# A two-layer Flamingo block on one core: the split context kept in DRAM between the layers

## The reference

```
layer 0: q, k, v = per-head 8x8 products of x, ctx, ctx     (16 heads of width 8)
         a = softmax(where(mask == 0, -1e20, q k^T) / sqrt(128));  h = a v Wo^T + bo
         x = x + tanh(g_xattn[0]) * h
         y = layernorm(x);  x = x + tanh(g_ffn[0]) * (shared_swiglu(y) + routed_swiglu(y, top 1 of 8))
layer 1: q = y Wq^T + bq,  k, v = ctx Wkv^T + bkv            (16 heads of width 64)
         x = x + tanh(g_xattn[1]) * (softmax(q k^T / 8) v Wo^T + bo)
         x = x + tanh(g_ffn[1]) * ffn(layernorm(x))          (ternary weights, 8-bit activations, width 512)
```

## Time and profile before

| | |
|---|---|
| median of 3 runs (lowest to highest) | 1311.85 us (1311.23 to 1313.99) |
| the profiled execution's own time | 1311.5 us |
| its span in the profile | 1309.6 us |
| PE busy / DVE / ACT / POOL | 87% / 70% / 55% / 43% of the span |
| DMA bytes moved | 137.91 MB |

### The profile page before, as it was taken

The page is one execution under the profiler, slowest core; times in us unless marked ns, Lnnn a source line. Parts: engine busy times, 40 slices in busy tenths (PEclk is TensorE's granted clock), DMA queues, the critical chain, the costliest instruction groups (busy, mean ns, idle before and its releaser), DMA issues.

```text
span 1309.6 us, 27739 instructions
## 1 busy us (share of the span) xinstructions
PE 1133.5 (87%) x10078; PEld 646.3 (49%) x10080; DVE 923.1 (70%) x1252; ACT 716.4 (55%) x983; POOL 560.2 (43%) x360
## 2 busy tenths in 40 slices
PE   0869899999999996887968899899999999999974
PEld 0335566566665655533424454544545454454542
DVE  6656666666666664777787767678686767777768
ACT  0525455555555545545666666566665656666642
POOL 5357766666666724234034323333333333333220
PEclk9979899999999999899999999999999999999996
DMA  5233334433443351000049878868677786867630
GB/s 157 71 91 82 82 97 106 119 80 101 107 112 81 83 146 38 1 21 27 1 73 141 147 154 141 161 135 156 135 148 154 139 156 136 162 135 136 119 68 14
DMA packets 256726, 137.91 MB, mean 105 GB/s; under 512 B 229184, under 2 KB 239920, under 8 KB 256672
## 3 DMA queue, kind: packets, MB, share of 16 engines
q1 hardware_dynamic: 250416, 134.03, 49.1%
q10 hardware_dynamic: 6256, 3.16, 1.0%
HBM read 49.64 MB, written 0.52 MB: 38 GB/s over the span
## 4 chain that ended last, share of the span: by engine, by line
PE 55%; DVE 12%; issue 9%; DMA 7%; SPq 6%; ACT 6%; ACTq 3%; POOL 1%; DVEq 0%; another core or an unknown queue 0%; POOLq 0%
PE bank L854 9%; PE bank L872 8%; PE bank L718 7%; PE bank L742 6%; DMA region<-u_w 5%; PE bank L746 5%; PE bank L759 4%; SPq L452 4%; PE bank L820 3%; DMA region<-wg_sb 3%; ACTq L384 3%; DVE region L1713 2%; DVE e_row L1522 2%; DVE neg_max L1561 2%; ACT region L1205 2%
## 5 line engine op out<-in xcount | busy, mean ns | idle before, releaser
L1522 DVE CUSTOM_DVE_ANT_0 e_row<-bank,region 112x1500 f32<-112x1500 f32 x128 | 220.1, 1720 | 125.4 <-PE bank L718 124.1
L1561 DVE TENSOR_REDUCE neg_max<-bank 128x1 f32<-128x1500 f32 x112 | 192.3, 1717 | 139.9 <-PE bank L854 139.9
L1205 ACT ACTIVATE region<-bank 125x896 f32<-125x896 f32 x192 | 176.0, 917 | 203.1 <-PE bank L746 203.0
L854 PE MATMUL bank<-region 128*128 128x500 f16 x1008 | 233.5, 377 | 3.3 <-ACT e_row L1232 1.8
L1241 ACT COPY region<-bank 128x768 f16<-128x768 f16 x224 | 178.2, 795 | 105.2 <-PE bank L820 105.2
L1232 ACT ACTIVATE e_row<-bank,neg_shift 128x1500 f32<-128x1500 f32 x112 | 169.4, 1513 | 84.5 <-DVE neg_shift L1565 84.3
L536 POOL CAST u_w<-e_row 128x1500 f16<-128x1500 f32 x56 | 81.8, 1461 | 210.9 <-ACT e_row L1232 210.9
L536 POOL CAST wg_sb<-e_row 128x1500 f16<-128x1500 f32 x56 | 82.5, 1473 | 201.4 <-ACT e_row L1232 156.5
L854 PEld LDWEIGHTS bank<-region 128*128 (+1 forms) x1008 | 96.8, 98 | 106.8 <-ACT e_row L1232 2.3
L742 PE MATMUL bank<-row_of,region 112*128 112x448 bf16 x384 | 138.1, 360 | 7.9 <-ACT region L1205 7.9
L746 PE MATMUL bank<-region 97*128 (+1 forms) x768 | 137.8, 260 | 0.0
(11 more groups left out here) (222 smaller groups left out, 1610.2 us busy)
## 6 DMA issues: line engine op xcount, KB each, us to landing
c_in<-in_ctx SPq DMA_DIRECT2D x32, 750.0 KB
region<-region SPq DMA_DIRECT2D x64, 192.0 KB, 2.8
region<-in_mask_Bx1xSxS_if SPq DMA_DIRECT2D x32, 328.1 KB
region<-region SPq DMA_DIRECT2D x64, 96.0 KB, 2.6
region<-region SPq DMA_DIRECT2D x8, 750.0 KB
g_w<-region SPq DMA_DIRECT2D x8, 750.0 KB
x_norm_t<-inverse_rows SPq DMA_DIRECT2D x16, 256.0 KB, 3.6
x_norm_t<-inverse_rows SPq DMA_DIRECT2D x16, 192.0 KB, 3.6
```

The costliest lines, as they stand in the source:

```text
L854: last = pe.matmul(score_banks1(par, t)[:, k, :], q1[:, ql, b, 128 * t:128 * (t + 1)], c_t1[par][:, cl, 4 * k:4 * k + 4, 0:KP], start=(ql ...
L1205: act.activation(p0[:, 2 * i:2 * i + 2, :], ring0("s", h, i)[0:KP, :, 0:HALF_ROWS], ACT.Exp, scale=SCALE0)\
L1522: dve.tensor_tensor_reduce(out=masked.rearrange("p (a k) -> p a k", a=3), in0=bank[0:R0, 0:3, 0:4 * KP], in1=mask_bias[par][:].rearrange(" ...
L1561: dve.tensor_reduce(neg_max[:, t:t + 1], score_banks1(par, t), AX.XY, ALU.max, negate=True)\
```

## The change

**Layer 0.** `c_split0` is laid out with all high columns of a chunk side by side, then all low ones. SP stores it, 750 KB a batch, to a DRAM scratch `split_rows` (`sync_split_out`, ahead of the load for batch b+2), and POOL's next split waits for that store. Each turned bank is now one half of all four groups, so a group needs both banks; the stacks are 12 DMAs of 32 rows, 8 after the first bank and 4 after the second, where they were 8 DMAs (64 and 32 rows); the bytes are the same.

**Layer 1.** The second load from `ctx`, ACT's and POOL's split, PE's 24 turns and DVE's two copies are gone. Instead `sync_split_in` loads both halves of batch b+2 from the scratch into `c_split1` at slot 3, and `sync_keep` loads those of batch b+1 from the scratch into `c_keep1` at slot 4, where it stood before. The context transpose of batch b+1 is issued ahead of slot 0 instead of after slot 2. The inverse's steps of both groups stand one slot earlier on PE and ACT (slots 4 and 0), and those of group 0 on SP too.

```diff
-        c_split0 = carve([128, KC, G, 2, 32], F16)
+        c_split0 = carve([128, KC, 2, G, 32], F16)
+        split_rows = nc.dram_tensor("split_rows", [B, KP, KC, 2, E], F16, kind="Internal").ap()
...
         def sync_stack(sp, b, par):
             wait_apart(sp, "sp", (sem("st0"), (b - 1) * (2 * NP)))
-            for g in range(G):
-                if g % 2 == 0:
-                    wait_apart(sp, "sp", (sem(f"ct_done0_{g // 2}"), b + 1))
-                rows = 64 * (g % 2)
-                sp.dma_start(c_stack[par][0:64, g], c_t0[rows:rows + 64, g // 2]).then_inc(sem(f"stack{par}_{g}"), 16)
-                sp.dma_start(c_stack[par][64:96, g], c_t0[rows:rows + 32, g // 2]).then_inc(sem(f"stack{par}_{g}"), 16)
+            for n in range(2):
+                wait_apart(sp, "sp", (sem(f"ct_done0_{n}"), b + 1))
+                for g in range(G):
+                    for at in ((0, 64), (32,))[n]:
+                        sp.dma_start(c_stack[par][at:at + 32, g], c_t0[32 * g:32 * g + 32, n])\
+                            .then_inc(sem(f"stack{par}_{g}"), 16)
+
+        def sync_split_out(sp, b):
+            wait_apart(sp, "sp", (sem("low0"), b + 1))
+            sp.dma_start(split_rows[b], c_split0[0:KP].rearrange("p c n g d -> p c n (g d)")).then_inc(sem("split_out0"), 16)
+
+        def sync_split_in(sp, b):
+            wait_apart(sp, "sp", (sem("c_turned1"), 16 * b))
+            sp.dma_start(c_split1[0:KP], split_rows[b]).then_inc(sem("split_in1"), 16)
...
         def sync_keep(sp, b, par):
-            wait_apart(sp, "sp", (sem("split_done1"), b + 1))
             wait_apart(sp, "sp", (sem("pv_done1"), 4 * (b - 1)))
-            sp.dma_start(c_keep1[par], c_split1[0:KP]).then_inc(sem("kept1"), 16)
+            sp.dma_start(c_keep1[par], split_rows[b]).then_inc(sem(f"kept1_{par}"), 16)
...
             def layer1(b, par, first, last):
-                if not (isinstance(b, int) and b + 2 >= B):
-                    sync_load_context(sp, 1, b + 2, par)
+                if not last:
+                    sync_turn_context1(sp, b + 1, 1 - par)
                 for t in range(T1):
                     sync_turn1(sp, b, par, t)
                     if t == 1 and not first:
                         sync_inverse_out1(sp, b - 1, 1 - par, 1)
                     if t == 2 and not first:
                         sync_inverse_back1(sp, b - 1, 1 - par, 1)
+                    if t == 4:
+                        sync_inverse_out1(sp, b, par, 0)
                     if t == 5:
-                        sync_inverse_out1(sp, b, par, 0)
-                    if t == 6:
                         sync_inverse_back1(sp, b, par, 0)
-                    if t == 2 and not last:
-                        sync_turn_context1(sp, b + 1, 1 - par)
+                    if t == 3 and not (isinstance(b, int) and b + 2 >= B):
+                        sync_split_in(sp, b + 2)
                     if t == GROUPS1[1][0] and not last:
                         sync_keep(sp, b + 1, 1 - par)
...
             low_weights(1)
             pool_rstd(pool, 1, TT, (0, TT))
-            pool_context1(pool, 0, 0)
             low_weights(2)
...
             def layer1(b, par, first, last):
                 for t in range(T1):
                     pool_high1(pool, b, par, t)
-                    if t == 2 and not last:
-                        pool_context1(pool, b + 1, 1 - par)
...
                 for t in range(T1):
-                    if t == 1 and not first:
+                    if t == 0 and not first:
                         act_inverse1(act, b - 1, 1)
-                    if t == 5:
+                    if t == 4:
                         act_inverse1(act, b, 0)
-                    if t == 1 and not last:
-                        act_split1(act, b + 1, 1 - par)
```

More of the change, by code:

```diff
@@ L223, in flamingo_kernel @@
         assert at[0] == split_at
-        c_split1 = carve([128, 2, KC, E], F16)
-        c_keep1 = [carve([128, 2, KC, E], F16)[0:KP],
+        c_split1 = carve([128, KC, 2, E], F16)
+        c_keep1 = [carve([128, KC, 2, E], F16)[0:KP],
                    g_w[:].rearrange("p e i -> p (e i)")[0:KP, 0:KC * E].bitcast(F16)
-                   .rearrange("p (n c e) -> p n c e", c=KC, n=2)]
-        c_t1 = [carve([128, 2, KC, 128], F16) for _ in range(2)]
+                   .rearrange("p (c n e) -> p c n e", c=KC, n=2)]
+        c_t1 = [carve([128, KC, 2, 128], F16) for _ in range(2)]
         GROUPS1 = [(0, 4), (4, T1)]
@@ L482, in layer0 @@
                         sync_load_mask(sp, b + 2)
+            sync_split_out(sp, 0)
             sync_stack(sp, 0, 0)
@@ L714, in pe_rows0 @@
             if t % 2 == 0:
-                pe.wait_ge(sem(f"stack{par}_{t // 2}"), per_use(b, par, 32))
+                pe.wait_ge(sem(f"stack{par}_{t // 2}"), per_use(b, par, 48))
             wait(pe, sem("max_done0"), b * T0 + t)
@@ L789, in pe_prep0 @@
                 last = pe.transpose(into[:, 128 * c:128 * (c + 1)],
-                                    c_split0[:, c, 2 * n:2 * n + 2].rearrange("p g two d -> p (g two d)"), ident16[:])
+                                    c_split0[:, c, n].rearrange("p g d -> p (g d)"), ident16[:])
             last.then_inc(sem("ct_turned0"), 1)
-        def pe_prep(pe):
-            for n in range(2):
-                pe.wait_ge(sem("split_done1" if n else "high1"), 1)
-                for c in range(KC):
-                    last = pe.transpose(pair_flat(n, F16)[:, 128 * c:128 * (c + 1)], c_split1[:, n, c, :], ident16[:])
-                last.then_inc(sem("ct_turned1"), 1)
         def projected1():
@@ L839, in pe_inverse1 @@
             pe.wait_ge(sem("inv_done1"), b * T1 + z)
-            pe.wait_ge(sem("high_copied1"), 2 * (b * T1 + (T1 if grp == 1 else GROUPS1[0][1])))
+            pe.wait_ge(sem("high_copied1"), 2 * (b * T1 + (T1 - 1 if grp == 1 and not (isinstance(b, int) and b == B - 1)
+                                                            else T1 if grp == 1 else 3)))
             if grp == 0 and isinstance(b, int) and b == B - 1:
-                pe.wait_ge(sem("residual"), 2 * TT + EARLY)
+                pe.wait_ge(sem("residual"), 2 * TT + 4)
             pe.transpose(inverse_turned()[0:z - a], row_inv[:, par, a:z], ident[:]).then_inc(sem("inverse_turned1"), 1)
@@ L846, in pe_scores1 @@
             if t == 0:
-                if isinstance(b, int) and b == 0:
-                    pe.wait_ge(sem("ct_done1"), 2)
-                else:
-                    pe.wait_ge(sem("c_turned1"), b * 16)
+                pe.wait_ge(sem("c_turned1"), 16 * (b + 1))
             wait(pe, sem("exp_done1"), b * T1 + t - 1)
@@ L868, in pe_pv1 @@
                 if grp == 0:
-                    pe.wait_ge(sem("kept1"), (b + 1) * 16)
+                    pe.wait_ge(sem(f"kept1_{par}"), per_use(b, par, 16))
             for c in range(first, end):
                 for cl, pl in ((0, 0), (0, 1), (1, 0)):
-                    last = pe.matmul(bank[:, U_BANK, 0:cols], c_keep1[par][:, cl, c, :], p1[grp][0:KP, pl, c, :],
+                    last = pe.matmul(bank[:, U_BANK, 0:cols], c_keep1[par][:, c, cl, :], p1[grp][0:KP, pl, c, :],
                                      start=(c == 0 and cl + pl == 0), stop=(c == KC - 1 and cl == 1))
@@ L1249, in act_inverse1 @@
             act.copy(inverse_row[0:z - a], inverse_turned()[0:z - a]).then_inc(sem("inverse_row1"), 1)
-        def act_split1(act, b, par):
-            act.wait_ge(sem(f"ctx_in1_{par}"), per_use(b, par, 16))
-            if not (isinstance(b, int) and b == 0):
-                act.wait_ge(sem("ct_turned1"), 2)
-                wait(act, sem("c_turned1"), 16 * (b - 1))
-                act.wait_ge(sem("kept1"), 16 * b)
-            act.copy(c_split1[0:KP, 0], c_in[par][:]).then_inc(sem("high1"), 1)
         def act_context0(act, b, par, n, place):
@@ L1262, in act_context0 @@
             if not (isinstance(b, int) and b == 0):
-                for g in (2 * n, 2 * n + 1):
-                    act.wait_ge(sem(f"stack{1 - par}_{g}"), per_use(b - 1, 1 - par, 32))
+                for g in range(G):
+                    act.wait_ge(sem(f"stack{1 - par}_{g}"), per_use(b - 1, 1 - par, 48))
             act.copy(c_t0[:, n].rearrange("p c k -> p (c k)"),
```

66 lines of the change are left out of this document (28 added, 38 removed).

## The result

| | before | after |
|---|---|---|
| median of the runs (lowest to highest) | 1312.31 us (1311.23 to 1313.99, 4 runs) | 1339.81 us (1332.96 to 1342.30, 4 runs) |
| the profiled execution's own time | 1311.5 us | 1342.3 us |
| its span | 1309.6 us | 1340.6 us |

The changed kernel is slower: the ratio is 1.020, with an interval of 1.0161 to 1.0239. The interval lies clear of 1, but whether the loss is more or less than 2% it leaves open. The forecast was 1279, with a range of 1258 to 1298.

A forecast was written before the change was run, and what follows sets the result against it. PE was taken to bound layer 1, with 5.6 us of waits per pair of batches. From 1311.5, layer 1 net -29.3 (-49.3 + 20.0), first FFN -3.3 and layer 0 nothing gave 1278.9, said as 1279; range 1258 to 1298.

The forecast's parts named there:

- The gain of layer 1: Layer 1: three waits vanish, 3.17 us in each of batches 2 to 14 (41.2) and 6.3 in batch 1.
- The wait inside `neg_shift`: Layer 1, slot 3: DVE's one-column addition waits 1.91 us during POOL's subtraction; removing it gains 1.80 us a batch.
- ACT's cast: Layer 1, slot 1: the context cast (1.47 us) stands ahead of copy and exponential; removing it gains .51 us a batch.
- the wait for turned tile 3: Layer 1: PE waits for tile 3's low half, its transpose queued behind the context's; removing this gains .86 us a batch.
- Tile 4's transpose lands at about 31.9, and tile 6's low half needs it at 31.7: the edge: Layer 1, us after slot 0's start: the transpose is .2 late, within the slack, so it costs nothing.
- Stalls after even batches too: Layer 1, a sign of error: if DVE's DMA wait stands after even batches too, the time is 1290 and more.
- the forecast's pattern: Layer 1: tile 5's transpose is 3.7 us late after odd batches only; PE loses 2.85 each, 7 x 2.85 = 20.0.
- I take 0: Layer 0: no net change, the new stacks and the 750 KB store being covered.
- The first FFN's start: DVE's seven normalizations lose POOL's subtraction beside them and end sooner; gain 3.3 us, between 0 and 5.4.
- PE's 24 turns ... give nothing; where they were on it, it would only be more gain: First FFN: batch 0's removed turns lie beside ACT's chain, so no gain; if on the chain, extra gain.
- The slower side: Rival in layer 1: scratch reads slower than copies inside SBUF; 1321 us at +1.5 us per transfer; chance .06.
- The collision is larger: Rival in layer 1: 1.6 us more for L416 and for L421, tile 5 up to 3.2 later; 1290 to 1309; chance .12.

The follow-up runs named there:

- e3: Changed kernel with layer 1's two scratch loads each issued in pieces of 112 and 13 rows at the same places; 1269.4 us, ratio .9669.
- e8: Kernel before the change, with only layer 1's context load and keep copy in pieces of 112 and 13 rows; 1304.5 us, ratio .9951.
- e5: Changed kernel with one more wait on SP: L421 is issued only when tile 4's transpose has landed; 1314.1 us in a single run.
- e2: Changed kernel with batch 0's store to the scratch held until ACT's last weight loads have landed; 1327.7 us, ratio 1.0121.
- e1: Changed kernel with load L416 moved from behind tile 3's transpose to behind tile 1's; 1278.9 us, ratio .9743.
- e4: Changed kernel with load L421 moved from slot 4 to slot 1 of the next batch, behind tile 1's transpose; 1277.1 us, ratio .9732.
- e11: Changed kernel, all 125-row transfers in two pieces, first store later, plus 24 unread unit-matrix turns on PE in the first FFN; 1256.7 us, ratio .9563.

## Why the prediction was wrong

- **The gain of layer 1 was right.** The forecast had 47.5 us for batches 1 to 14; the profile after shows 47.4 outside slot 0, and e3 45.6 in all. The wait inside `neg_shift`, ACT's cast and the wait for turned tile 3 are all gone. e8 and e3 show that the splits were most of it. That it fits to .1 us is partly luck: slots 1 and 5 gain more than forecast, and slots 2, 4 and 6 of even batches are each .2 to .25 longer than before, which the forecast did not have.
- **The step that failed** is "Tile 4's transpose lands at about 31.9, and tile 6's low half needs it at 31.7: the edge". It landed 39.05 us after slot 0 (943.45 to 982.50). Of the 7.1 us between, 1.9 are that L416 itself was issued later, at 23.0 and not 21.1, behind the stalled slot 0; the rest is that the transpose landed 16.1 us after L416 and not 10.75. The sum took the transfer behind which the transpose is issued and left out the one issued 3.8 us after it, as if what is issued later could not hold it. The updates in the trace and e5 show that this doesn't hold here: L421 holds the rest of a transpose that was issued ahead of it. How it does so stays open.
- **Its consequences** were three. The late tile is 4 and not 5, so that both parities are hit (43.3 us of waits over eight batches, where 3.7 after each second one was forecast). The wait of 5.3 to 5.7 us exceeds what DVE's slack covers. And PE's wait is long enough here for the granted clock to fall, 2.6 us more per even batch, of which the forecast had nothing. 72.0 us stand where the forecast had 20.0. Stalls after even batches too were among the prediction's own signs of being wrong. e5, which takes away L421's reach, gives the forecast's pattern (tile 5, only after odd batches from batch 5 on); its size, 5.2 to 5.6 us for 2.85, comes from L421's later issue and from the clock.
- **Layer 0 was not neutral.** "I take 0" looked at the steady batches, where the change costs under .1 us each (26.39 and 25.75 against 26.31 and 25.68). At the start the first store meets the weight loads and costs 6.4 us (e2). The other 1.4 us of layer 0 are near what executions differ by: the same code of layer 0 takes 399.9 us up to batch 15 in e1, 401.1 in e4 and 401.3 in the changed kernel.
- **The first FFN's start**: the normalizations fell from 7.33 to 4.53 us, 2.8 where 3.3 was forecast. Then the stage lost 3.7 us behind them. "PE's 24 turns ... give nothing; where they were on it, it would only be more gain" was wrong in sign: e11 gives back 3.1 us in the profile. The 3.7 is one execution's size; without the turns it is between .6 and 4.2.
- **The rivals.** The slower side was forecast by slower reads. That isn't what happened: by the updates L416 lands 8.4 to 9.0 us after its issue, and the copy inside SBUF of before landed 9.0 to 9.6 after its own (953.69 to 962.81 is 9.1); e1 and e4 read the same bytes from the scratch and are 61 to 63 us faster. "The collision is larger" had the place, but its upper end of 1309 was too low; by its own terms it is 1278.9 + 22.4 + 14 = 1315. It looked for more of the same price, SP held longer behind one transfer, and SP was held less: tile 4's transpose ended on SP at 972.30, 5.9 us after L416's issue where 6.8 was forecast. The chance of .06 for slower was too small for a change that put two transfers of which the sum knew only single instances so near each other.

The sum with measured terms: 1311.5 - 47.4 - 2.3 (batch 0) + 72.0 + 6.4 + 1.4 - 2.6 + 3.7 = 1342.7, against 1342.3. These terms are the stages of the table above added up, so that they meet the total is no test of the causes.

## What to carry to other kernels

Before moving a large transfer, look at how many DMA engines it uses (its DMA share while it runs alone), and cut a transfer of an awkward row count into pieces that use all of them; here 112 + 13 instead of 125 rows turned a loss of 27 us into a gain of 44. A cost read at one large transfer on a queue can't be used twice when two come close: look at what a following one does to a small transfer issued ahead of it. And read the start and the small stages of a kernel as carefully as its loop: a store that nothing there was waiting for held up the weights, and work taken off PE in a gap let the clock stay low.

## What the runs showed of the hardware

- A DMA transpose stood 2.9 us behind one narrow transfer (125 rows, DMA share .31 alone) and 3.8 us ahead of another. Five of its sixteen updates came at 976.6 to 976.7 and eleven at 982.4 to 982.5, with the second transfer. With the second held back until the transpose was through, all sixteen came within .15 us. Why the eleven wait was not found.
- In pieces of 112 and 13 rows, the second transfer was again issued while the transpose was in flight, and the transpose landed 3.6 us ahead of it (e3, 935.36 and 938.93).
- A wait added to SP made the kernel about 26 us faster (e5 against the changed kernel).
- After 5.03 us without work PE ran 5.2 us at .51 of its clock; after 4.11 us (e5) it ran 4.3 us at .60; after 1.47 us it stayed at 1.00.
- A DVE low half took 2.77 to 2.98 us beside POOL's cast, and 1.72 otherwise.
- 24 turns that nobody reads shortened their stage by 3.1 us in the profile, in step with 10.1 us less at the lower level of the clock.
